# Attention values multiplied as fp32 instead of split halves, and one statistics pass over two interleaved heads

## The reference

```
q  = LN(fp8_linear(ln(x), wq))  ; k = LN(fp8_linear(ln(x), wk)) ; v = fp8_linear(ln(x), wv)
core = softmax(q k^T / sqrt(128)) v              # 16 query heads, 8 key/value heads, head size 128
qx = LN(fp8_linear(ln(x), wqx)) ; kx, vx = split(ctx @ w_kv_x^T) ; kx = LN(kx)
xout = softmax(qx kx^T / sqrt(128)) vx
y  = x + tanh(g) * (fp8grid(concat(core, xout) / smooth) @ wproj^T) * scales
```

## Time and profile before

| | |
|---|---|
| median of 3 runs | 554.91 us (548.64 to 555.04) |
| the profiled execution, its time | 553.87 us |
| its span, first to last instruction | 552.1 us |
| PE busy | 435.9 us (79%), 3238 matmul records |
| DVE busy | 405.2 us (73%) |
| ACT busy | 309.9 us (56%) |
| POOL busy | 293.5 us (53%) |
| granted TensorE clock, mean | 0.925 of full |

### The profile page before, as it was taken

How to read it: one execution, slowest core, us unless ns; L and a number is a source line. 1 busy time by engine, 2 the same in 40 slices (tenths; PEclk the granted TensorE clock), 3 DMA queues, 4 the chain that set the end, 5 groups by cost and what they waited for, 6 DMA issues and landing times.

```text
span 552.1 us, 10895 instructions
## 1 busy us (share of the span) xinstructions
PE 435.9 (79%) x3238; PEld 314.1 (57%) x3238; DVE 405.2 (73%) x1071; ACT 309.9 (56%) x642; POOL 293.5 (53%) x546
## 2 busy tenths in 40 slices
PE   0457875989898988998898989888878779999940
PEld 0323553656565655665565656565668658787830
DVE  4757756688989889889898888989976655222245
ACT  2456775567776676776775677668783031333320
POOL 1028354385576575676568566666562046046670
PEclk9977887899999999999999999999987678999985
DMA  8900029999900000000000000000048012334407
GB/s 212 313 27 2 0 35 193 305 293 292 267 4 0 0 0 0 0 0 0 0 0 0 0 0 0 0 2 1 2 170 345 2 57 95 98 92 128 123 25 228
DMA packets 34812, 45.68 MB, mean 83 GB/s; under 512 B 3034, under 2 KB 32223, under 8 KB 33888
## 3 DMA queue, kind: packets, MB, share of 16 engines
q1 hardware_dynamic: 26656, 35.61, 21.1%
q0 software_dynamic: 6992, 9.46, 7.8%
q10 hardware_dynamic: 1136, 0.27, 0.3%
HBM read 28.34 MB, written 24.32 MB: 95 GB/s over the span
## 4 chain that ended last, share of the span: by engine, by line
PE 57%; DVE 15%; ACT 11%; issue 7%; DMA 7%; POOL 1%; ACTq 1%; SPq 0%; POOLq 0%; DVEq 0%
PE proj_ps L852 12%; PE score_ps L875 8%; PE proj_ps L1004 8%; PE out_ps L911 6%; PE proj_ps L844 6%; PE headT_ps L866 4%; ACT qT L681 4%; DMA wp_sb<-in_wpT 3%; ACT vf L652 3%; DMA rowv<-in_rowc 2%; PE pv_ps L900 2%; DVE ys L1197 2%; DVE yv L1251 2%; PE pv_ps L902 1%; PE pv_ps L901 1%
## 5 line engine op out<-in xcount | busy, mean ns | idle before, releaser
L852 PE MATMUL proj_ps<-arena 128*128 128x512 f16 x384 | 103.3, 397 | 5.2 <-DMA wp_sb<-in_wpT 4.6
L1220 DVE BATCH_NORM_STATS2 st<-rot 128x6 f32<-128x128 f32 x384 | 83.0, 279 | 30.8 <-ACT rot L644 29.3
L866 PE MATMUL headT_ps<-idf,rot 128*128 128x128 f32 x384 | 60.2, 280 | 32.8 <-ACT qT L681 30.6
L644 ACT ACTIVATE rot<-proj_ps 128x512 f32<-128x512 f32 x96 | 57.0, 594 | 50.5 <-PE proj_ps L852 46.5
L866 PEld LDWEIGHTS headT_ps<-idf,rot 128*128 128x128 f32 x384 | 44.5, 142 | 56.5 <-issue 39.1
L520 POOL TENSOR_TENSOR rot<-rot,cw 128x512 f32<-128x512 f32 x64 | 70.5, 1122 | 2.5
L875 PEld LDWEIGHTS score_ps<-kT,qT 128*128 128x128 f32 x512 | 65.3, 203 | 8.1 <-ACT qT L681 5.1
L531 POOL TENSOR_TENSOR reg<-reg,rinv 128x512 f32<-128x512 f32 x32 | 33.4, 1042 | 63.8 <-DVE rinv L1244 63.8
L875 PE MATMUL score_ps<-kT,qT 128*128 128x64 f32 x512 | 65.2, 284 | 0.0
L852 PEld LDWEIGHTS proj_ps<-arena 128*128 (+1 forms) x384 | 38.8, 106 | 35.2 <-issue 12.3
L681 ACT ACTIVATE qT<-headT_ps,colv 128x512 f32<-128x512 f32 x64 | 49.3, 770 | 12.2 <-PE headT_ps L866 12.2
(11 more groups left out here) (226 smaller groups left out, 929.6 us busy)
## 6 DMA issues: line engine op xcount, KB each, us to landing
zbuf<-fill SPq DMA_DIRECT2D x1, 16576.5 KB, 61.1
arena<-in_wffn SPq DMA_DIRECT2D x4, 1536.0 KB, 12.4
arena<-zbuf SPq DMA_DIRECT2D x32, 128.5 KB, 2.1
wkv_stage<-in_wkvN SPq DMA_DIRECT2D x1, 2048.0 KB, 15.1
wp_sb<-in_wpT POOLq DMA_DIRECT2D x1, 2048.0 KB, 15.6
wp_sb<-ybuf SPq DMA_DIRECT2D x8, 256.0 KB, 4.5
xs<-in_x SPq DMA_DIRECT2D x2, 512.0 KB, 5.1
wp_sb<-in_wqN POOLq DMA_DIRECT2D x1, 1024.0 KB, 12.9
```

Source lines behind the costliest of these rows:

```text
L644: act.activation(raw[c % 2][i], proj_ps[i % 2][:, :], ACT.Copy).then_inc(proj_evac, 1)
L852: mm = pe.matmul(ps, lhs, w[kind][:, ch, 512 * b:512 * b + 512], start=(k == 0), stop=(k == 3))
L866: mm = pe.transpose(dst, raw[c % 2][i][:, h * D:(h + 1) * D], idf[:, :])
L1220: ins = ve.bn_stats(st[:, 4 * i + h, :], raw[c % 2][i][:, h * D:(h + 1) * D])
```

## The change

Four things are changed together.

- The values are kept as one fp32 buffer `vv`, written by one ACT operation (`values_out`); the fp16 copies `vh`, `vl16`, the ACT operation L655 and POOL's `values_low` are gone.
- The transposed probabilities are copied as fp32 by ACT (`prob_copy`, the former L691); DVE's `prob_low` is gone, and V waits for ACT's copy alone.
- V is 8 fp32 matmuls in place of 24 fp16 ones.
- One statistics operation takes two heads, read in turn (element 0 of head h, element 0 of head h+1, element 1 of head h, ...), so its even half is one head and its odd half the other. `variance` on POOL then has two operations in place of six; what it leaves out is the mean term, since the mean is zero.

```diff
-            def values_high(t, c):
+            def values_out(t, c):
                 n = NU * t + c
                 act.wait_ge(proj_done, 4 * n + 4)
-                ge(act, v_lo, n - 1)
+                ge(act, pv_done, n - 3)
                 scale = col("s_v") if c < 2 else 1.0 / WKV_SCALE
-                act.activation(vf[:, c % 2, :], proj_ps[1][:, :], ACT.Copy, scale=scale).then_inc(v_full, 1)
-                act.wait_ge(v_full, n + 1)
-                ge(act, pv_done, n - 3)
-                act.activation(vh[:, c, :], vf[:, c % 2, :], ACT.Copy).then_inc(v_hi, 1)
+                act.activation(vv[:, c, :], proj_ps[1][:, :], ACT.Copy, scale=scale).then_inc(v_full, 1)
...
-                gp.tensor_tensor(vw[:, 0, :], st[:, :, 2], st[:, :, 5], ALU.add)
-                chained(achain, gp.tensor_tensor(vw[:, 1, :], st[:, :, 1], st[:, :, 1], ALU.mult), 3 * n + 1)
-                gp.tensor_tensor(vw[:, 0, :], vw[:, 0, :], epsc[:, x, :], ALU.add)
-                chained(achain, gp.tensor_scalar(vw[:, 2, :], vw[:, 1, :], float(D), None, ALU.mult), 3 * n + 2)
-                gp.tensor_tensor(va[:, :], vw[:, 2, :], vw[:, 0, :], ALU.add).then_inc(var_done, 1)
+                gp.tensor_tensor(va[:, :], st[:, :, 2], epsc[:, x, :], ALU.add).then_inc(var_done, 1)
...
-            def values_low(t, c):
-                n = NU * t + c
-                gp.wait_ge(v_hi, n + 1)
-                gp.tensor_tensor(vl16[:, c, :], vf[:, c % 2, :], vh[:, c, :], ALU.subtract).then_inc(v_lo, 1)
...
-                pe.wait_ge(prob_lo, w + 1)
-                pe.wait_ge(v_lo, w + 1)
+                pe.wait_ge(prob_out, w + 1)
+                pe.wait_ge(v_full, w + 1)
...
-                        o = pv_ps[b][:, g * P:(g + 1) * P]
-                        lo = 512 + g * P
-                        vhi, vlo = vh[rows, u, g * D:(g + 1) * D], vl16[rows, u, g * D:(g + 1) * D]
-                        pe.matmul(o, vhi, pT[rows, g * P:(g + 1) * P], start=True, stop=False)
-                        pe.matmul(o, vhi, pT[rows, lo:lo + P], start=False, stop=False)
-                        mm = pe.matmul(o, vlo, pT[rows, g * P:(g + 1) * P], start=False, stop=True)
+                        mm = pe.matmul(pv_ps[b][:, g * P:(g + 1) * P], vv[rows, u, g * D:(g + 1) * D],
+                                       pT[rows, g * P:(g + 1) * P], start=True, stop=True)
...
             def stats(n, c, i):
                 ve.wait_ge(proj_evac, 3 * n + i + 1)
-                for h in range(4):
-                    ins = ve.bn_stats(st[:, 4 * i + h, :], raw[c % 2][i][:, h * D:(h + 1) * D])
+                for h in range(0, 4, 2):
+                    ins = ve.bn_stats(st[:, 4 * i + h:4 * i + h + 2, :].rearrange("p h s -> p (h s)"),
+                                      raw[c % 2][i][:, h * D:(h + 2) * D].rearrange("p (h d) -> p d h", d=D))
...
-            def prob_low(w, s):
-                ve.wait_ge(prob_hi, w + 1)
-                ve.tensor_tensor(probT[s][:, 512:1024], probT_ps[:, :], probT[s][:, 0:512],
-                                 ALU.subtract).then_inc(prob_lo, 1)
...
-                if live(n, 3):
-                    prob_low(n - 3, (c - 3) % 2)
                 if proj:
                     stats(n, c, 0)
```

More of the change, by code:

```diff
@@ L163, in build @@
         kT = sb("kT", [P, 2, 4, P], F32)
-        vf = sb("vf", [P, 2, 512], F32)
-        vh = sb("vh", [P, NU, 512], F16)
-        vl16 = sb("vl16", [P, NU, 512], F16)
+        vv = sb("vv", [P, NU, 512], F32)
         wkv_stage = sb("wkv_stage", [P, 4096], F32)
@@ L173, in build @@
         ctx_st = reg2[:, :]
-        probT = [reg2[:, 512 * i:512 * i + 512].bitcast(F16) for i in range(2)]
+        probT = [reg2[:, 512 * i:512 * i + 512] for i in range(2)]
         catq = [reg2[:, 1024 + 512 * i:1536 + 512 * i].bitcast(BF16) for i in range(2)]
@@ L193, in build @@
         NLH = 12
-        st = sb("st", [P, NLH, 6], F32)
-        vw = sb("vw", [P, 3, NLH], F32)
+        st = sb("st", [P, NLH, 3], F32)
+        vw = sb("vw", [P, NLH], F32)
         va = sb("va", [P, NLH], F32)
@@ L342, in build @@
         probn_done = sem("probn_done")
-        prob_hi = sem("prob_hi")
-        prob_lo = sem("prob_lo")
+        prob_out = sem("prob_out")
         v_full = sem("v_full")
-        v_hi = sem("v_hi")
-        v_lo = sem("v_lo")
         probT_done = sem("probT_done")
@@ L495, in variance @@
                 ge(gp, coef_done, n)
-                gp.tensor_tensor(vw[:, 0, :], st[:, :, 2], st[:, :, 5], ALU.add)
-                chained(achain, gp.tensor_tensor(vw[:, 1, :], st[:, :, 1], st[:, :, 1], ALU.mult), 3 * n + 1)
-                gp.tensor_tensor(vw[:, 0, :], vw[:, 0, :], epsc[:, x, :], ALU.add)
-                chained(achain, gp.tensor_scalar(vw[:, 2, :], vw[:, 1, :], float(D), None, ALU.mult), 3 * n + 2)
-                gp.tensor_tensor(va[:, :], vw[:, 2, :], vw[:, 0, :], ALU.add).then_inc(var_done, 1)
+                gp.tensor_tensor(va[:, :], st[:, :, 2], epsc[:, x, :], ALU.add).then_inc(var_done, 1)
                 gp.wait_ge(var_done, n + 1)
-                gp.tensor_tensor(vw[:, 1, :], va[:, :], newt[:, 0, :], ALU.mult).then_inc(achain, 1)
+                gp.tensor_tensor(vw[:, :], va[:, :], newt[:, 0, :], ALU.mult).then_inc(achain, 1)
             def coefficients(n):
-                gp.wait_ge(achain, 3 * n + 3)
+                gp.wait_ge(achain, n + 1)
                 gp.wait_ge(root_done, n + 1)
-                chained(nchain, gp.tensor_tensor(nw[:, 0, :], vw[:, 1, :], r0[:, :], ALU.mult), 3 * n + 1)
+                chained(nchain, gp.tensor_tensor(nw[:, 0, :], vw[:, :], r0[:, :], ALU.mult), 3 * n + 1)
                 chained(nchain, gp.tensor_tensor(nw[:, 1, :], nw[:, 0, :], r0[:, :], ALU.mult), 3 * n + 2)
@@ L545, in step @@
                     norm_bank(n, c, 2)
-                    values_low(t, c)
                 if c == 0 and live(n, -NU):
@@ L686, in expo, with prob_copy @@
                 act.activation(prob[s], prob[s], ACT.Exp, scale=SCORE_SCALE).then_inc(exp_done, 1)
-            def prob_high(w, s):
+            def prob_copy(w, s):
                 act.wait_ge(probT_done, w + 1)
                 ge(act, pv_done, w - 1)
-                act.activation(probT[s][:, 0:512], probT_ps[:, :], ACT.Copy).then_inc(prob_hi, 1)
+                act.activation(probT[s], probT_ps[:, :], ACT.Copy).then_inc(prob_out, 1)
             def step(t, c):
@@ L708, in step @@
                 if proj:
-                    values_high(t, c)
+                    values_out(t, c)
                 if heads:
@@ L712, in step @@
                 if attend:
-                    prob_high(n - 2, c % 2)
+                    prob_copy(n - 2, c % 2)
                 if heads:
@@ L880, in prob_transposes @@
                 pe.wait_ge(probn_done, w + 1)
-                ge(pe, prob_lo, w)
+                ge(pe, prob_out, w)
                 for g in range(4):
```

## The result

| | before | after |
|---|---|---|
| first comparison, median | 552.48 us (548.64 to 555.04, 4 runs) | 532.24 us (530.03 to 535.09, 4 runs) |
| ratio, 95% interval | | 0.9665 [0.9608, 0.9722] |
| a later comparison, median | 555.50 us (550.08 to 557.64, 7 runs) | 535.77 us (534.53 to 539.62, 4 runs) |
| ratio, 95% interval | | 0.9684 [0.9590, 0.9778] |
| profiled execution, span | 552.1 us | 528.2 us |

The changed kernel is 3.2 to 3.4% faster. 536.5 was forecast; it took 532.2 in one comparison and 535.8 in the other. As a difference 17.3 us was forecast, and 20.2 and 19.7 were measured. The profile of after is the fastest of its four executions, so from here on each stretch is read in two profiles of each kernel.

What follows compares the result with a forecast made beforehand. The loop was taken to run at PE's pace plus stalls at T2 and V; 13.5 us from six passes, 1.9 last tile, 0.5 ahead of the loop and 1.4 drain total 17.3, from 553.9 to about 536.5 us, range 528 to 560.

Steps and rivals of the forecast that it cites:

- The stall at T2: PE idle before T2, waiting for ACT's qT behind the values copy: 0.65 us less in c = 3, 0.5 in c = 0.
- The stall at V: PE's 1.66 us wait for L1226 in c = 2 goes, part moves to T1; c = 1 and 2 gain 1.7 us.
- V's own price: V's fp32 matmuls on PE, paired in 8 slots of 0.11 us: 0.98 up to O, 0.2 more per step.
- Statistics: DVE's two-head operations: 0.74 us per bank, 0.13 less than before, assuming the interleaved read runs at full rate.
- upper bound of the statistics: DVE at half rate, read from L1201's 1284 against 692 ns: a bank takes 1.29 us.
- POOL: Removing POOL's L526 and four small operations per step gives nothing, as it already waits 7.7 us a pass for ACT's root.
- Before the loop: The stretch ahead of the loop: PE's 4.57 us wait for output weights swallows the first steps' gains, but for 0.5 us.
- The last tile's 1.9: Last tile, without a grid pass: shorter T2 waits and 0.44 us of a V wait, less 4 x 0.2, give 1.9 us.
- The drain's 1.4: In the drain, L1251 starts 2.2 us earlier; two V's at half clock cost 0.4 each: net 1.4 us.
- Slow statistics: Rival: the interleaved read doubles DVE's time per column, 0.55 us more per bank, 544 us; chance 0.32 with pairing.
- V without pairing: Rival: V's halves don't pair on PE, 16 slots, 0.88 us more per step than forecast, 559 us; chance 0.2.
- the stall goes altogether: Rival: DVE's lateness does not return at T1, 4.6 us gained per pass, 522 us; chance 0.05, shared with another clock pattern.

Runs made afterwards that it cites:

- act_back: The changed kernel with the fp32 to fp16 copy of the value bank put back on ACT ahead of H1, result unused; 551.34 us, a pass of 44.34.
- no_collide: The changed kernel with POOL's scalings in steps with c = 1 held until DVE's grid pass is done; 533.05 us, ratio 0.9634, a pass of 42.04.
- pool_back: The changed kernel with four small operations and a bank subtraction put back on POOL, on spare buffers; 537.85 us, a pass of 42.69.
- before_again: The kernel before, unedited, profiled a second time; 557.42 us in a single run.
- stats_contig: The changed kernel with each statistics operation reading its two heads one after the other, variances then wrong; 535.69 us, a pass of 42.62.
- v_one_half: The changed kernel with both sequences' V matmuls on rows 0 to 63, so they can't pair; 560.02 us, a pass of 45.41.
- o_late: The changed kernel with output product O moved behind the probability transposes, except in c = 2; 522.71 us, ratio 0.9444, a pass of 40.36.
- values_only: The changed kernel with the old statistics and variance, keeping fp32 values and probabilities; 543.65 us, ratio 0.9833, a pass of 42.86.
- stats_only: The kernel before with only the paired statistics and short variance, values still split fp16; 558.01 us against 554.78, ratio 1.0074.

## Why the prediction was right, point by point

**The stall at T2: right.** In c = 3 it fell from 1.23 to 0.57 us (0.65 predicted), in c = 0 from 0.96 to 0.43 (0.5). In c = 1 the idle time in front of T2 did not fall, 0.53 and 0.52, but 0.24 of waiting ahead of the probability transposes went and T2 stands 1.59 us behind T1's start where it stood 2.06. `act_back` undid it.

**The stall at V: right.** It went, and a wait of T1 in c = 2 came (0.64, predicted 0.5), with 0.20 at the probability transposes that was not named. Over c = 1 and 2, 1.7 less 0.2 was predicted; 2.06 less the net gains of c = 3 and c = 0 (0.66 - 0.31 and 0.53 - 0.31) leaves 1.5.

**V's own price: too low.** The term that was mis-sized is "8 slots of 0.11". V takes 1.09 us up to O, 0.31 over before in place of 0.2. Pairing costs nothing: the slots are 0.11 apart as forecast, but the first one takes 0.21, with pairs and without them. In the rows of the fold, from which the pace was taken, the first slot is no longer than the rest; what makes it longer in V no run here shows. That is 0.1 in each of the three steps where it counts, and of the pass's 2.25 it leaves about 2.0 (2.06 measured; predicted pass 42.5, measured 42.64).

**Statistics: the price right, the worth not foreseen.** 0.75 us per bank, 0.74 predicted. But the 0.26 per pass that I credited them with depend on where POOL's scalings fall: alone they cost 0.14, with the values part they give 0.22.

**One row was misread.** For the upper bound of the statistics I took L1201's 1284 against 692 ns as two forms of an operation. They are one operation, with and without POOL at work beside it: with POOL held back (`no_collide`) all eight take 0.69. The bound was kept in the range and decided nothing, but the row held the collision, which is worth 0.6 us per pass.

**POOL: right.** Covered, as `pool_back` shows (0.05).

**The sum.** Six passes were put at 13.5: 6 x 2.06 = 12.4, the first of them ahead of the first residual. The rest is counted from T2 to T2 of the steps with c = 3, behind which a residual stands 2.19 us after and 1.64 before. Before the loop 0.5: 2.9 + 0.55 - 2.06 = 1.4 by the means of two profiles, whose own scatter is 1.3 and 1.9. The last tile's 1.9: 1.5. The drain's 1.4 needs its own working. From T2 to the last residual `before_again` takes 4.37 us more. The chain of waits in its drain, and then that of after:

```profile
436.76 0.26 DVE arena L1364
437.01 0.61 DVE reg L1226
437.67 0.29 PE pv_ps L900 x2
```

```profile
416.94 0.26 DVE arena L1336
417.20 1.21 DVE yv L1225 x2
```

L1226 and the wait for V between the routing work and the division are gone, 2.26 us (2.2 predicted), and 0.76 behind it, where O stood behind a late V and behind L1004, both at half clock, so that this is partly the clock's; against it 0.3 for the slower V in front. The late V itself ran at half clock too, its 12 slots 0.11 apart where they are 0.056 at full clock, which is 0.65 of the 2.26; the 2.2 of the prediction holds a V at that pace as well. The remaining 1.65 is the clock: two groups of matmuls ran at half clock in `before_again` (L927 1.94 in place of 1.09 us, the scores 2.74 in place of 1.90). So the mechanism gave 1.3 to 2.7, where 1.4 was predicted.

PE's timelines, `before_again` and then after, for these two groups:

```profile
412.80 1.94 PE L927 MATMUL proj_ps<-idf,wkv_stage 128*128 128x128 f32 x8 [1.71 <-ACT wkv_stage L738]
414.53 2.74 PE L875 MATMUL score_ps<-kT,qT 128*128 128x64 f32 x16
```

```profile
394.33 1.09 PE L905 MATMUL proj_ps<-idf,wkv_stage 128*128 128x128 f32 x8 [1.71 <-ACT wkv_stage L720]
395.26 1.90 PE L857 MATMUL score_ps<-kT,qT 128*128 128x64 f32 x16
```

In all the mechanisms give 12.4 + 1.4 + 1.5 + (1.3 to 2.7) = 16.6 to 18.0 us, where 17.3 was forecast. That the sum comes so near is partly luck: the ground ahead of the loop gave more than forecast, the passes and the last tile less. The two pairs of profiles differ by 22.7 us on average, the medians by 20.2 and 19.7. The rest, 2 to 6 us, is in the profiles time at half clock that before had and after had not: 1.6 in the loop, 1.7 to 4.8 in the drain besides what lies in the working above. The prediction had put the clock down only as what could spoil it. Whether the change takes these stretches away, or whether they would come back in other executions, the two profiles of each kernel can't say.

**The rivals.** Slow statistics are out by `stats_contig`, and V without pairing by `v_one_half`, which also shows that its price was right in the passes (2.77 us, 2.65 predicted) and in the last tile (45.46 against 41.91, 3.5 predicted). In the drain it was 1.3 in place of 3.4, and ahead of the first residual this run took 4 us more than its longer pass explains, for which the rival had no term. (That rival's 0.8% is over the median 554.9; over the profiled execution it is 1.0.) That the stall goes altogether (522 us) did not happen either, though 522.7 is what `o_late` took: the time was there, and it needed a second edit in PE's order to reach it.

## What to carry to other kernels

When one change lightens several engines, ask of each what waits for it. Here the copy on ACT and the slot on DVE each held PE up at a place that the timeline shows, and an equal relief of POOL gave nothing. Matmuls that use half of the rows and come in pairs make fp32 cheap enough to save the split into high and low parts (0.3 us more on PE against a conversion on ACT and a subtraction each on DVE and POOL); without the pairs it would have lost. A part can show most of the gain per pass and little over half of it in the total, as `values_only` does, so read both. And before trusting two means of one operation as two "forms", look at what runs on the other engines at that time.

## What the runs showed of the hardware

**VectorE and GpSimd slow each other down.** An operation of DVE with both inputs in SBUF takes 0.69 us alone, 1.28 when POOL is already scaling banks, and 1.58 when both start together; POOL's two scalings take 2.04 alone, 2.92 beside it. POOL's two scalings one by one, after and then in `stats_only`:

```profile
246.60 1.48 POOL L511 TENSOR_TENSOR rot<-rot,cw 128x512 f32<-128x512 f32 x1
248.04 1.48 POOL L511 TENSOR_TENSOR rot<-rot,cw 128x512 f32<-128x512 f32 x1
```

```profile
212.09 1.04 POOL L516 TENSOR_TENSOR rot<-rot,cw 128x512 f32<-128x512 f32 x1
```

These rows look like turns, not like two engines that both run slower. Whoever starts first keeps its time alone: DVE's L1175 at 246.49 takes 0.69, POOL's scaling at 212.09 takes 1.04. The other ends behind it by its own time alone less 0.14: DVE 0.55 us behind POOL (248.62 - 248.08 after, 213.68 - 213.13 in `stats_only`), POOL 0.90 behind DVE (248.08 - 247.18 and 249.52 - 248.62).

A subtraction with one input in PSUM isn't touched (0.68 in the earlier trace rows and in `stats_only`); the same with both in SBUF is (0.70 to 1.52). An operation with a single bf16 input can be hit as well. Timelines of DVE and of POOL after, in the drain:

```profile
401.42 1.63 DVE L1168 TENSOR_SCALAR yv<-yv 128x1024 bf16<-128x1024 bf16 x1
```

```profile
401.30 1.47 POOL L542 COPY wkv_stage<-wkv_stage 128x1536 f32<-128x1536 f32 x1
```

It takes 0.43 us everywhere else in these timelines; here it starts 0.12 after POOL's copy and ends 0.28 behind it, which is 0.43 less 0.15: a turn again. The Trainium skill says of GpSimd, in "GPSIMD Engine Reference", section 8, "Key points", that its SBUF interfaces are shared with VectorE, with contention when VectorE has two SBUF inputs or runs in a two-port mode. These rows agree, and give the price.

**Paired fp32 matmuls.** Two streams of fp32 matmuls with 64 rows each take 1.09 us for 16 records of 128 columns; one after the other on the same rows they take 1.98. That is 0.89 us, 45%, for giving each its own half of the array. Behind the first slot one stream starts a record every 0.11 us, and two streams start two.
